# Regrouping tap logits, token transposes and small exponentials in a convolution and mixture-of-experts kernel

## The reference, cut to what matters

```
avg, mx = mean and max over the pixels of each channel
wt = (mx @ w2.T + b2) - (avg @ w1.T + b1)      # 128 x 9 taps per image
wt = softmax(wt, axis=1)  of shape (b*c, 1, 3, 3)   # over an axis of length one
y  = depthwise conv(x, wt, padding 1) + bias + x
```

## Time and profile before

| | us |
|---|---|
| median of 3 runs | 1534.79 (1530.91 to 1535.08) |
| the profiled execution's own time | 1534.89 |
| its span, first to last instruction | 1532.4 |
| TensorE busy, whole span | 1453.9 (95%) |
| VectorE busy | 1308.8 (85%) |
| ScalarE busy | 1096.7 (72%) |
| POOL busy | 961.6 (63%) |

### The profile page before, as it was taken

How to read it: one execution, slowest core, us unless ns; L and a number is a source line. 1 busy time by engine, 2 the same in 40 slices (tenths; PEclk the granted TensorE clock), 3 DMA queues, 4 the chain that set the end, 5 groups by cost and what they waited for, 6 DMA issues and landing times.

```text
span 1532.4 us, 45755 instructions
## 1 busy us (share of the span) xinstructions
PE 1453.9 (95%) x12204; PEld 1114.6 (73%) x12205; DVE 1308.8 (85%) x2676; ACT 1096.7 (72%) x2514; POOL 961.6 (63%) x1069
## 2 busy tenths in 40 slices
PE   5999999999999867999999999999999999999996
PEld 2345454555545433999999999999999999999995
DVE  2468888888888984999999999999989999999995
ACT  5477777878777523777777777777777777777773
POOL 2004455545555674777777777777777777777773
PEclk8899999999999955999999999999999999999998
DMA  4211212121222127111111232223232322222222
GB/s 141 74 38 57 70 63 81 63 75 58 77 69 64 40 71 151 41 47 40 44 43 57 66 93 86 92 86 93 85 94 83 92 86 91 84 86 78 78 75 109
DMA packets 85647, 115.77 MB, mean 76 GB/s; under 512 B 17613, under 2 KB 69865, under 8 KB 85590
## 3 DMA queue, kind: packets, MB, share of 16 engines
q1 hardware_dynamic: 64886, 76.83, 17.0%
q0 software_dynamic: 18112, 34.27, 7.0%
q10 hardware_dynamic: 2592, 4.00, 0.9%
HBM read 60.08 MB, written 58.48 MB: 77 GB/s over the span
## 4 chain that ended last, share of the span: by engine, by line
POOL 38%; PE 24%; issue 23%; DVE 6%; ACT 4%; DMA 2%; POOLq 2%; SPq 1%; ACTq 0%; DVEq 0%
PE psV L902 14%; POOL token_out L542 14%; POOL xn L530 14%; POOL yt L537 9%; PE psA L840 4%; PE psV L849 3%; DVE x L1235 2%; POOL rows_by_pair L512 1%; ACT cv L628 1%; PE psT L884 1%; ACT diag L618 1%; PE psG L886 1%; DMA stage<-in_L_ffn_W_dram 1%; ACT lnv L601 1%; POOLq L542 1%
## 5 line engine op out<-in xcount | busy, mean ns | idle before, releaser
L1495 DVE TENSOR_TENSOR gl<-g,gh 128x512 f16<-128x512 f32 x620 | 489.1, 828 | 71.1 <-ACT gh L777 61.2
L512 POOL DMA_INDIRECT rows_by_pair<-rows,idx x256 | 263.6, 1030 | 318.7 <-issue 196.1
L542 POOL DMA_INDIRECT token_out<-yt,rt x310 | 338.7, 1093 | 184.7 <-POOL yt L537 133.6
L902 PE MATMUL psV<-lp,diag 128*128 128x512 f32 x576 | 274.4, 613 | 20.5 <-ACT cv L628 20.5
L777 ACT ACTIVATE gh<-g 128x512 f16<-128x512 f32 x465 | 274.5, 624 | 16.8
L770 ACT ACTIVATE g<-psT 128x512 f32<-128x512 f32 x310 | 182.2, 597 | 101.3 <-PE psT L1057 74.4
L770 ACT ACTIVATE g<-psV 128x512 f32<-128x512 f32 x310 | 184.8, 597 | 90.1 <-PE psV L1057 62.0
L530 POOL TENSOR_SCALAR xn<-rt 128x128 f32<-128x128 f32 x310 | 221.5, 721 | 14.0 <-DMA rt<-rows_by_pair 10.1
L1078 PE MATMUL psR<-wall,gh 128*128 x1240 | 221.3, 273 | 0.4 <-DVE ya L1512 0.4
L1078 PE MATMUL psG<-wall,gh 128*128 x1240 | 221.3, 273 | 0.0
L902 PEld LDWEIGHTS psV<-lp,diag 128*128 128x128 f32 x576 | 106.2, 193 | 150.9 <-issue 108.2
(11 more groups left out here) (231 smaller groups left out, 2950.2 us busy)
## 6 DMA issues: line engine op xcount, KB each, us to landing
rt<-rows_by_pair SPq DMA_DIRECT2D x155, 133.0 KB, 2.1
xb<-in_x_dram SPq DMA_DIRECT2D x32, 512.0 KB, 3.5
yq<-token_out SPq DMA_DIRECT2D x112, 128.0 KB, 2.4
out_dram<-oq SPq DMA_DIRECT2D x112, 128.0 KB
token_out<-yt,rt POOLq DMA_INDIRECT x310, 2.3
rows_by_pair<-rows,idx POOLq DMA_INDIRECT x256, 2.4
stage<-in_L_ffn_W_dram SPq DMA_DIRECT2D x1, 2048.0 KB, 8.3
ye<-token_out SPq DMA_DIRECT2D x4, 512.0 KB, 4.3
```

Source lines behind the costliest of these rows:

```text
L512: gp.indirect_dma_start(rows_dram, bass.IndirectOffsetOnAxis(ap=idx[p][:, b:b + 1].bitcast(U32), axis=0), rows[p][:, b, :], None).then_inc ...
L542: gp.indirect_dma_start(y_dram, bass.IndirectOffsetOnAxis(ap=rt[r][:, b, ID:ID + 1].bitcast(U32), axis=0), yt[r][:, b, :], None, bounds_ch ...
L902: ins = te.matmul(psConv.rearrange("p (h w) -> p h w", w=WW), diag[k][:, m, :], lp[j][:, y:y + HH // 2, dx:dx + WW], start=(m == 0), stop= ...
L1495: v.tensor_tensor(gl[side][q][:, cols], g[side][:, cols], gh[side][q][:, cols], ALU.subtract).then_inc(lo_done, 1)
```

## The change

- TensorE makes the 36 products of the tap logits in one go, behind the last tap of the convolution and ahead of both halves of the next `centre`.
- A block of tokens is one product: the moving operand `turn_w` is the identity and the nine gate columns side by side (137 columns), where there were a transpose and a product. A PSUM bank holds three such blocks; the eight lie in the three banks of `psTG` (the former `psT` and `psG`). ScalarE's copies of the negated gate sums and means (all nine columns now, into `neg`) and of the tokens are in two parts each, as the blocks lie. VectorE's `shifts` reads the gate sums from `neg` in SBUF; TensorE no longer waits for `lg_ready`.
- Image 0's blocks: six at the start of the step, two behind the first half of its convolution. Two taps of the convolution go ahead of the second variance.
- ScalarE: `sum_up` of image 0 goes behind `token_std` and `keep`; the exponential of the tap softmax goes ahead of the second `take` of image 1.
- VectorE: `own_places` no longer waits for itself at once; the wait is behind `split_pooled`. The sum of the two weights (`den`) goes ahead of the wait for the rows' buffer.

```diff
@@ PSUM and buffers @@
-        psT = psum("psT", 1024)
-        psG = psum("psG", 512)
+        psTG = psum("psTG", 1536)
+        psT, psG = psTG[:, 0:1024], psTG[:, 1024:1536]
...
+        turn_w = sb("turn_w", [P, P + G], held=phase_a)
+        wgc = turn_w[:, P:P + G]
+        neg = [sb(f"neg{p}", [P, NB2, G], held=phase_a) for p in range(2)]
...
+        TW = P + G
+        PER = HALF // TW
+        turned = lambda b: psTG[:, HALF * (b // PER) + TW * (b % PER):HALF * (b // PER) + TW * (b % PER + 1)]
+        turned_parts = ((0, 2 * PER, psT.rearrange("p (n c) -> p n c", n=2)[:, :, 0:PER * TW].rearrange("p n (b t) -> p n b t", t=TW)),
+                        (2 * PER, NBLK, psG[:, 0:(NBLK - 2 * PER) * TW].rearrange("p (n b t) -> p n b t", n=1, t=TW)))
@@ ScalarE @@
-                sc_.activation(negm[...], psG[...][:, k * NBLK:(k + 1) * NBLK, E], ACT.Copy, scale=-1.0).then_inc(stat_ready, 1)
+                for first, end, part in turned_parts:
+                    last = sc_.activation(neg[...][...], part[:, :, :, P:TW], ACT.Copy, scale=-1.0)
+                last.then_inc(stat_ready, 1)
...
-                sc_.activation(rows[p][:, blks, 0:D], psT[:, :].rearrange("p (b d) -> p b d", d=D), ACT.Copy, scale=0.5)
+                for first, end, part in turned_parts:
+                    sc_.activation(rows[p][...], part[:, :, :, 0:P], ACT.Copy, scale=0.5)
...
-                    if st_.on(1):
+                    if k == 1 and st_.on(1):
                         sum_up(st_, k)
                     if st_.on(3):
                         token_std(st_, k)
                         keep(st_, k)
+                    if k == 0 and st_.on(1):
+                        sum_up(st_, k)
+                    if k == 1 and st_.on(1):
+                        act.wait_ge(z_ready, st_.count(1, 1, 1))
+                        sc_.activation(ez[:, :, :], zd[:, :, :], ACT.Exp).then_inc(ez_ready, 1)
                     if st_.on(2):
                         take(st_, k, 1)
...
-                if st_.on(1):
-                    act.wait_ge(z_ready, st_.count(1, 1, 1))
-                    sc_.activation(ez[:, :, :], zd[:, :, :], ACT.Exp).then_inc(ez_ready, 1)
@@ TensorE @@
-                    if k == 0 and (not st_.fixed or st_.count(3, 1, 0) > 0):
-                        pe.wait_ge(lg_ready, st_.count(3, 1, 0))
...
-                    te.transpose(psT[:, b * P:(b + 1) * P], x1[j][:, b * P:(b + 1) * P], ident[:, :])
-                    at = (k * NBLK + b) * G
-                    last = te.matmul(psG[:, at:at + G], x1[j][:, b * P:(b + 1) * P], wgc[:, :], start=True, stop=True)
+                    last = te.matmul(turned(b), x1[j][:, b * P:(b + 1) * P], turn_w[:, :], start=True, stop=True)
...
-                        turn(st_, k, 0, TURN_1)
+                        turn(st_, k, 0, TURN_1 if k else TURN_0)
...
-                    if st_.on(3):
+                    if k == 1 and st_.on(3):
                         turn(st_, k, TURN_1, NBLK)
...
-                        conv(st_, k, 0, 0)
+                        for m in range(2):
+                            conv(st_, k, 0, m)
...
+                    if k == 0 and st_.on(3):
+                        turn(st_, k, TURN_0, NBLK)
...
-                for quarter in range(4):
-                    if quarter < 2:
-                        if st_.on(2):
-                            conv(st_, 1, 1, N_PE - 2 + quarter)
-                    elif st_.next().on(1):
-                        centre(st_.next(), 0, quarter - 2)
-                    if st_.on(1):
-                        tap_logits(st_, quarter)
+                if st_.on(1):
+                    tap_logits(st_)
+                if st_.next().on(1):
+                    for h in range(2):
+                        centre(st_.next(), 0, h)
@@ VectorE @@
+                v.tensor_copy(turn_w[:, 0:P], ident[:, :])
...
-                v.tensor_tensor(lg[:, :, :], gates[:, :, 0:E], spread(rstd[p]), ALU.mult).then_inc(lg_ready, 1)
+                v.scalar_tensor_tensor(out=lg[:, :, :], in0=neg[p][:, :, 0:E], scalar=-1.0, in1=spread(rstd[p]), op0=ALU.mult, op1=ALU.mult).then_inc(lg_ready, 1)
...
-                c4.link(v.tensor_tensor(pos[:, :, :], pos[:, :, :], pairs[:, :, :], ALU.mult))
+                c4.mark(v.tensor_tensor(pos[:, :, :], pos[:, :, :], pairs[:, :, :], ALU.mult))
...
-                link(v.tensor_reduce(idf[:, :], pos[:, :, :], AX_X, ALU.add))
+                c4.wait()
+                c4.mark(v.tensor_reduce(idf[:, :], pos[:, :, :], AX_X, ALU.add))
+                dve.wait_ge(e2_ready, st_.count(4, 1, 1))
+                c4.link(v.tensor_tensor(den[:, :], e2[:, :, 0], e2[:, :, 1], ALU.add))
```

More of the change, by code:

```diff
@@ L81, in conv_moe_block @@
     TURN_1 = 5
+    TURN_0 = 6
     UP_A = 2
@@ L229, in conv_moe_block @@
         tln = sb("tln", [P, NBLK])
-        negm, rstd, nmr = ([sb(f"{n}{p}", [P, NB2]) for p in range(2)] for n in ("negm", "rstd", "nmr"))
+        rstd, nmr = ([sb(f"{n}{p}", [P, NB2]) for p in range(2)] for n in ("rstd", "nmr"))
         lg, lg2, eq, sc, m1h, m2h, mh = (sb(n, [P, NB2, E]) for n in ("lg", "lg2", "eq", "sc", "m1h", "m2h", "mh"))
@@ L635, in token_std @@
                     act.wait_ge(lg_ready, st_.count(3, 1, 0))
-                sc_.activation(negm[st_.slot(3)][:, k * NBLK:(k + 1) * NBLK], psG[:, 0:NB2 * G].rearrange("p (b g) -> p b g", g=G)[:, k * NBLK:(k + 1) * NBLK, E],
-                               ACT.Copy, scale=-1.0).then_inc(stat_ready, 1)
+                for first, end, part in turned_parts:
+                    last = sc_.activation(neg[st_.slot(3)][:, k * NBLK + first:k * NBLK + end, :].rearrange("p (n b) g -> p n b g", b=part.shape[2]),
+                                          part[:, :, :, P:TW], ACT.Copy, scale=-1.0)
+                last.then_inc(stat_ready, 1)
                 act.wait_ge(stat_ready, n)
                 for b in range(NBLK):
-                    last = sc_.activation(spent[:, b * P:(b + 1) * P], psT[:, b * P:(b + 1) * P], ACT.Square, bias=negm[st_.slot(3)][:, k * NBLK + b:k * NBLK + b + 1],
+                    last = sc_.activation(spent[:, b * P:(b + 1) * P], turned(b)[:, 0:P], ACT.Square, bias=neg[st_.slot(3)][:, k * NBLK + b, E:G],
                                           accum_out=ssq[:, b:b + 1])
@@ L653, in keep @@
                 blks = slice(k * NBLK, (k + 1) * NBLK)
-                sc_.activation(rows[p][:, blks, 0:D], psT[:, :].rearrange("p (b d) -> p b d", d=D), ACT.Copy, scale=0.5)
+                for first, end, part in turned_parts:
+                    sc_.activation(rows[p][:, k * NBLK + first:k * NBLK + end, 0:D].rearrange("p (n b) d -> p n b d", b=part.shape[2]),
+                                   part[:, :, :, 0:P], ACT.Copy, scale=0.5)
                 act.wait_ge(rstd_ready, st_.count(3, 2, k + 1))
@@ L856, in setup_done, with tap_logits @@
                 pe.wait_ge(s_setup_dve, 2)
-            def tap_logits(st_, quarter):
-                if quarter == 0:
-                    pe.wait_ge(pool16_ready, st_.count(1, 1, 1))
-                    if st_.on(4):
-                        pe.wait_ge(rank_read, st_.count(4, 1, 1))
-                for tap in range(TAPS * quarter // 4, TAPS * (quarter + 1) // 4):
+            def tap_logits(st_):
+                pe.wait_ge(pool16_ready, st_.count(1, 1, 1))
+                if st_.on(4):
+                    pe.wait_ge(rank_read, st_.count(4, 1, 1))
+                for tap in range(TAPS):
                     at = R_TAP + 4 * tap
@@ L955, in step @@
                     if st_.on(2):
-                        for m in range(len(taps_pe[0]) if k == 0 else N_PE - 2):
+                        for m in range(len(taps_pe[k])):
                             conv(st_, k, 1, m)
@@ L1248, in shifts @@
                 dve.wait_ge(rstd_ready, st_.count(3, 2, 2))
-                v.tensor_tensor(nmr[p][:, :], negm[p][:, :], rstd[p][:, :], ALU.mult)
-                v.tensor_tensor(lg[:, :, :], gates[:, :, 0:E], spread(rstd[p]), ALU.mult).then_inc(lg_ready, 1)
+                v.tensor_tensor(nmr[p][:, :], neg[p][:, :, E], rstd[p][:, :], ALU.mult)
+                v.scalar_tensor_tensor(out=lg[:, :, :], in0=neg[p][:, :, 0:E], scalar=-1.0, in1=spread(rstd[p]), op0=ALU.mult, op1=ALU.mult).then_inc(lg_ready, 1)
             def first_choice(st_):
```

10 lines of the change are left out of this document (2 added, 8 removed).

## The result

| | before | after |
|---|---|---|
| median, us | 1533.7 (4 runs, 1530.91 to 1535.08) | 1510.22 (4 runs, 1509.31 to 1511.81) |
| ratio to before, 95% interval | | 0.985, 0.9833 to 0.9868 |
| the profiled execution's own time | 1534.89 | 1511.81 |
| its span | 1532.4 | 1510.0 |
| TensorE, VectorE, ScalarE, POOL busy | 1453.9, 1308.8, 1096.7, 961.6 | 1431.3, 1305.5, 1101.1, 966.1 |

The kernel is faster by 23 us.

A forecast was written before the change was run, and what follows sets the result against it. TensorE looked like the bound, but VectorE's wait for the last tap logit closed the loop. Twelve steps of 1.32 us plus 3.3 made 19.1, the tail 0.3: 1534.9 - 19.1 - 0.3 = 1515.5 us, range 1511 to 1522.

The forecast's parts named there:

- Part 1: TensorE's tap logits ahead of the next centring: last logit 1.97 us earlier, VectorE's 1.43 us wait gone.
- Part 2: TensorE's token blocks as one 137-column product: 0.235 us each, 0.8 us less TensorE work a step.
- rival A: TensorE becomes the bound if a token block costs 0.41 us: period 31.0, 1532 us; chance 4%.
- Part 3: ScalarE's exponential ahead of its last copy: VectorE isn't held; TensorE's variance waits 0.4 us, out of 2 us of slack.
- Part 4: ScalarE's copies of means and rows split in two: the extra means copy adds 0.1 us a step.
- Part 5: VectorE reaches its shift 0.4 us earlier but finds rstd late: nothing in a step; gate sums from SBUF, nothing.
- Part 6: Image 0's new order: its token chain starts about 1 us earlier on ScalarE; nobody waits for it, no gain given.
- the first three softmaxes: Start of the loop: the first pair gives nothing, the second and third steps together 3.3 us.
- The tail: POOL's scatters behind the steps follow VectorE's last row write: 0.3 us gained; expert phase 0, with +-2 us.
- B: ScalarE's row copy of image 0 waits for earlier scatters; every other step loses 0.7 us: 1521 us; chance 10%.
- C: TensorE's clock falls to half inside the steps, slower from two stretches a step: 1557 us at three; chance 5%.
- D: Logits don't decide: rstd or the exponential comes 0.5 us later than reckoned, steps give 0.8: 1523 us; chance 8%.

The follow-up runs named there:

- split_prod: Changed kernel with each 137-column product taken apart into transpose and gate product, ScalarE's copies in one part each; 1510.04 us, ratio 0.9852.
- more_1: Changed kernel with four idle 128x18 copies on ScalarE ahead of image 1's squares in every step; 1512.78 us, ratio 0.9867.
- order0: Changed kernel with image 0's old order on TensorE, and its sum ahead of its squares on ScalarE; 1519.06 us, ratio 0.9899.
- split_order0: Changed kernel with both the merged product taken apart and image 0 in its old order; 1522.1 us, ratio 0.9917.
- dve_order: Changed kernel with VectorE's old order: it waits for its own places at once, sum of weights last; 1512.19 us, ratio 0.9857.
- first_step: Kernel before with the tap logits in one go in its first step alone; 1532.1 us, ratio 0.9993.
- logits_exp: Kernel before with the tap logits in one go and the exponential ahead of ScalarE's last copy; 1522.37 us, ratio 0.9926.
- quarters: Changed kernel with the tap logits in quarters again, two of them behind the halves of the centring; 1530.86 us, ratio 0.999.

## Why the prediction was nearly right, and where it failed

**Part 1, logits in one go: right.** The wait is gone from all middle steps and nothing took its place at the softmax.

**Part 2, the product of 137 columns: the price right, the use wrong.** Instructions 0.116 us apart, 0.23 a block against 0.235; rival A fell with it. The distance is that of the streamed columns alone, so the weight loads hide behind so short a stream. The Trainium skill (TensorE: Matmul & The Clock Gate, LDWEIGHTS) gives P/1.2 ns for a load, by estimate 107 ns here, which fits; the agreement is one of figures only, as the trace records each of these loads as 0.19 us long and one starting every 0.117. But that TensorE's work fell by 0.8 us was worth nothing measurable with the order of image 0 in place (*split_prod*).

**Part 3, the exponential: right** in its waits (0.28 us of VectorE's at L1222, nothing beyond). That TensorE's first variance waits for the square happened too. The step that failed is its end, "which comes out of its 2 us of slack". The slack at the point where TensorE is needed, the copy of image 1's first half, was 0.2 to 0.3 us (*more_1*: 0.17; *order0*: the copy 0.69 later behind the softmax, the sum 0.43), not 1.6: the slack counted over a whole step lies partly ahead of the pin at 2.65 us and partly in the hole at the copy, where in this order of work only blocks of image 0 fill it.

**Part 4, copies in two parts: right in place and in size.** The way from the sum to the first square grew by 0.11 us (1.25 to 1.36) against 0.1. 0.04 of that is there with one copy of nine columns instead of one (*split_order0*), 0.07 is the second copy.

**Part 5, VectorE's order and operands: right.** Worth nothing in a step (*dve_order*), and VectorE waits 0.33 to 0.46 for rstd in the loop's steps and 0.75 in the written-out ones, against 0.4 to 0.6. Gate sums read from SBUF (L1256) take 0.28 us, as from PSUM in the earlier trace rows: the 62 cycles of the Trainium skill (VectorE: DVE Perf Modes, The TRN2 errata), by estimate 65 ns, don't show in this row. The form of the instruction changed with the operand, so the cleaner pair is L1250 and L1257 of the earlier trace rows, one form and both 0.28.

**Part 6, the order of image 0: wrong.** "Nobody waits for it" overlooked that TensorE's hole is on a path: the prediction's last sentence there, "The two blocks fill TensorE's wait for the copy", named two thirds of what brings 0.42 to 0.62 us a step (0.46 of 0.70; the rest is the block that moved ahead of the variance), and gave it no price. The period was reckoned as if TensorE were never late, and with this part it isn't: that it came out at 29.74 against 29.76 is in part luck. Undone alone in the reckoning it would have cost nothing, and on the chip it costs a third of the gain.

**The sum.** The term that was most in error is the one for the first three softmaxes: 3.3 us in the forecast, 5.8 in the profiles. The new period was forecast at 29.76 and is 29.74. A step gave 1.42, not 1.32: from the shift to the softmax it is 1.49 less in the mean of the steps (1.79 to 0.30), where the wait as the profile gives it, 1.42, leaves 0.07 of that out; the shift follows rstd 0.04 sooner; 0.11 go to the copies. (The prediction's own two ends, 31.12 and 29.76, give 1.36, not 1.32.) That is 17.1 against 15.8. For the first three softmaxes the step that failed is "5.1 is the first pair's ... so it gives nothing": in the pair of profiles it gave 2.4, of which 0.7 comes from the earlier work and 1.7 from a half-clock stretch that isn't there (*first_step*); whether that stretch went by the change or by chance stays open. The other 3.4 are near the 3.3 given for the second and third. The two terms were 1.3 and 2.5 too small. The tail came as forecast at VectorE (0.27 against 0.3); POOL's pace took 1.2 back, the expert phase and the time around the span gave 1.1, neither for a cause that a run shows. So the profiled execution came to 1511.8 where 1515.5 was forecast. The last 1.6 us are its distance to the median, and no mechanism: the forecast started from 1534.9, and with a fourth run the median before is 1533.7. The low end of the range had left 4.5 us for the first and third step to give more; together with what has no mechanism the result was 5.3 below the forecast.

**The rivals.** A and B didn't happen (a block costs 0.23; L666 waits for scatters once in the whole kernel, 2.0 us, as L654 did before with 2.2). C, a clock that falls inside the steps, neither: the granted clock is 1.00 from 43 to 493 us. D is in a way what *order0* and *logits_exp* show: rstd late by 0.4 to 0.75 us, with 1519 to 1522 us against the 1523 given.

## What to carry to other kernels

Slack summed over a step of a pipeline says little: take it at the place where the next engine needs the result, behind the last point that pins the engine. A removed wait is worth what lies up to the next wait in the chain, here four instructions further, so two moves can be worth 11 us together and little singly: the logits alone gave 2.9, and the whole change gave 1.5 without the logits and 4.8 without the exponential. And a hole in an engine that is waiting for a copy is a cheap place for work that nobody is waiting for; filling it beyond its length (six squares against two) gave part of the gain back.

## What was not expected of the hardware

- Of the 2.4 us between the profiles of *before* and *first_step*, 1.7 lie in a stretch at half clock: 0.57 in the mean between 58 and 62 us. Such a stretch is there in four of fourteen profiles, somewhere from 55 to 62 us. TensorE's busy time in the 4 us ahead of it was 2.11 us with it (*before*) and without (*first_step*, *after*).
- A small copy of ScalarE behind another costs 0.065 us from start to start (four of 128x18 in 0.26), less than the 0.10 between a 128x8 copy and its neighbour in the earlier trace rows.
- POOL's pace of scatters in the tail varied from 1.341 (*quarters*) to 1.368 us (*after*) with the same code on POOL, worth 1.7 us over 63 scatters. Its cause stays open.
